# A running sum whose flag is replaced by a second address read from a table

## The reference

```python
q, k, v = x @ Wq + bq, x @ Wk + bk, x @ Wv + bv      # 6250 nodes, 8 heads of 32
e = edge_attr @ We                                    # 106250 edges, sorted by dst
alpha = sum_c(q[dst] * (k[src] + e)) / sqrt(32)
ea = exp(alpha - segment_max(alpha, dst)[dst])
denom = segment_sum(ea, dst)
out = segment_sum((v[src] + e) * ea / denom[dst], dst) + x @ Ws + bs
```

## Time and profile before

| | us |
|---|---|
| median of 3 runs | 2572.81 (2572.0 to 2574.0) |
| the profiled execution: its own time | 2570.37 |
| the profiled execution: first to last instruction | 2568.6 |
| busy: PE | 2382.9 |
| busy: DVE | 2037.0 |
| busy: POOL | 1811.8 |
| busy: ACT | 1577.5 |

### The profile page before, as it was taken

The page is one execution under the profiler, slowest core; times in us unless marked ns, Lnnn a source line. Parts: engine busy times, 40 slices in busy tenths (PEclk is TensorE's granted clock), DMA queues, the critical chain, the costliest instruction groups (busy, mean ns, idle before and its releaser), DMA issues. The chain is left out here.

```text
span 2568.6 us, 67072 instructions
## 1 busy us (share of the span) xinstructions
PE 2382.9 (93%) x13310; PEld 1992.2 (78%) x13311; DVE 2037.0 (79%) x5261; ACT 1577.5 (61%) x4373; POOL 1811.8 (71%) x2136
## 2 busy tenths in 40 slices
PE   6998999999999999999999999999995657999998
PEld 2445788888888888888888888888883646999998
DVE  6865899999999999999999999999997773222222
ACT  1222677777777677777767777767774224666665
POOL 4123788888888888888888888888886104666666
PEclk9999999999999999999999999999998557999999
DMA  7326777777777777777777777777772753433443
GB/s 229 128 107 187 231 227 221 227 228 228 223 227 227 220 230 224 221 227 226 227 221 226 227 225 229 227 218 220 228 223 78 227 162 60 71 63 64 70 66 55
DMA packets 337693, 476.68 MB, mean 186 GB/s; under 512 B 61318, under 2 KB 268492, under 8 KB 337052
## 3 DMA queue, kind: packets, MB, share of 16 engines
q0 software_dynamic: 92576, 259.72, 37.8%
q1 hardware_dynamic: 238492, 213.23, 28.0%
q10 hardware_dynamic: 6288, 0.05, 0.1%
HBM read 425.40 MB, written 50.57 MB: 185 GB/s over the span
## 5 line engine op out<-in xcount | busy, mean ns | idle before, releaser
L809 POOL DMA_INDIRECT kv_ring<-vk_table,tab_c x880 | 860.6, 978 | 284.3 <-issue 208.2
L963 PE MATMUL ps_e<-we_sb,aT 128*128 128x256 f32 x3520 | 919.5, 384 | 27.9 <-DVE ve_ke L1050 21.6
L963 PEld LDWEIGHTS ps_e<-we_sb,aT 128*128 128x128 f32 x3520 | 601.0, 191 | 102.8 <-issue 48.6
L1044 DVE TENSOR_TENSOR ve_ke<-kv_ring,ps_e 128x512 f32<-128x512 f32 x880 | 599.9, 682 | 38.1 <-PE ps_e L967 24.0
L1014 PE MATMUL ps_u<-ve_ke,sel 128*128 128x264 f32 x1760 | 547.7, 393 | 20.3 <-DVE node_slots L1114 6.8
L819 POOL TENSOR_TENSOR ve_ke<-ve_ke 128x256 f32<-128x256 f32 x880 | 553.4, 633 | 18.5 <-ACT factor L936 4.9
L967 PE MATMUL ps_e<-q_slots,selT 128*128 x1760 | 517.6, 375 | 0.0
L896 ACT COPY aT<-ps_t 128x256 f32<-128x256 f32 x880 | 325.5, 370 | 310.1 <-PE ps_t L951 189.6
L1114 DVE SCALAR_TENSOR_TENSOR node_slots<-node_slots,same_tile,ps_u 128x264 f32 x880 | 423.0, 481 | 29.5 <-DVE node_slots L1099 10.6
L967 PEld LDWEIGHTS ps_e<-q_slots,selT 128*128 128x128 f32 x1760 | 335.1, 190 | 45.9
L1032 DVE TENSOR_REDUCE alpha<-ve_ke 128x8 f32<-128x256 f32 x880 | 365.3, 415 | 5.6 <-issue 3.6
(11 more groups left out here) (249 smaller groups left out, 2642.3 us busy)
## 6 DMA issues: line engine op xcount, KB each, us to landing
a_ring<-in_edge_attr SPq DMA_DIRECT2D x880, 128.0 KB
loc_c<-loc_table SPq DMA_DIRECT2D x220, 128.0 KB
kv_ring<-vk_table,tab_c POOLq DMA_INDIRECT x880
vk_table<-kv_out SPq DMA_DIRECT2D x49, 256.0 KB
skip_table<-skip_out SPq DMA_DIRECT2D x49, 128.0 KB
skip<-skip_table SPq DMA_DIRECT2D x7, 896.0 KB, 10.8
xn_table<-node_slots SPq DMA_DIRECT2D x7, 896.0 KB, 6.5
out<-node_slots SPq DMA_DIRECT2D x1, 6144.0 KB
```

What stands on the lines that cost most here:

```text
L809: g.indirect_dma_start(out=kv_ring[:, i % N_KV, :], out_offset=None, in_=vk_table, in_offset=bass.IndirectOffsetOnAxis(ap=tab_c[:, c % N_T ...
L963: t.matmul(ps_e[i % 2][:, 0:D], aT[i % 2][:, k * P:(k + 1) * P], we_sb[:, k, :], start=(k == 0), stop=(k == KD - 1))
L1044: v.tensor_tensor(ve_ke[:, to:ke + 1:ke - to, 0:D], kv.rearrange("p (t d) -> p t d", t=2), e[:, None, :].to_broadcast([P, 2, D]), ALU.add) ...
```

## The change

The add becomes a plain addition. Its first operand gets an address of its own: the slot of the item's node tile where that tile goes on, and an area of 264 zeros behind the last slot where an item is the first of its node tile. The address comes from a second table of one number per item, `item_sums_from`, kept in another partition of the same tile as the first table. The register read between L1044 and L1032 is done twice per item, once for each table. `same_tile` is still made, later in the first stage, since the new table and the softmax need it; the new table takes two more operations there, and POOL clears the zeros once. `block_expert` moves into a free row of the same tile.

```diff
+        item_sums_from = item_rows[64:65, :]
...
-            q_slots = sb("q_slots", [P, NT + 2, SLOT], F32R, first_use)
-        node_slots = sb("node_slots", [P, NT + 2, SLOT])
+            q_words = sb("q_words", [P, (NT + 2) * SLOT + UW], F32R, first_use)
+        sums_flat = sb("node_words", [P, (NT + 2) * SLOT + UW])
+        ZEROS = NT + 2
...
+                g.memset(sums_flat[:, ZEROS * SLOT:], 0.0).then_inc(first_cleared, 1)
...
                 def masks(step):
                     if step == 0:
                         dve.wait_ge(turned_copied, IB)
+                        v.memset(same_tile[:, 0:1], 0.0)
+                        v.tensor_tensor(same_tile[:, 1:IT], node_tile_rep[:, 1:IT], node_tile_rep[:, 0:IT - 1], ALU.is_equal)
...
                     elif step == 2:
                         v.tensor_tensor(mask, m_lo, m_hi, ALU.add).then_inc(tables_ready, 1)
+                        dve.wait_ge(tables_ready, MASK)
+                        then(v.scalar_tensor_tensor(out=t_rep[:, :], in0=node_tile_rep[:, :], scalar=-float(ZEROS), in1=same_tile[:, :],
+                                                    op0=ALU.add, op1=ALU.mult))
+                        v.tensor_scalar(item_sums_from, t_rep[64:65, :], float(ZEROS), None, ALU.add)
...
-                def add(c, i, n, before):
+                def sums_from(c, i):
+                    return dve.value_load(item_sums_from[0:1, bass.ds(c * CH + i, 1)], min_val=0, max_val=ZEROS)
+
+                def add(c, i, n):
                     m = c * CH + i
-                    to, sofar = [sums_flat[:, bass.ds(k * SLOT, UW)] for k in (n, before)]
+                    to, sofar = [sums_flat[:, bass.ds(k * SLOT, UW)] for k in n]
                     dve.wait_ge(s["summed"], at("summed", m))
                     dve.wait_ge(s["acc_added"], at("acc_added", m - 1))
-                    v.scalar_tensor_tensor(out=to, in0=sofar, scalar=same_tile[:, m:m + 1], in1=ps_u[i % 2][:, 0:UW], op0=ALU.mult, op1=ALU.add
-                                           ).then_inc(s["acc_added"], 1)
+                    v.tensor_tensor(to, sofar, ps_u[i % 2][:, 0:UW], ALU.add).then_inc(s["acc_added"], 1)
...
-                            tiles.append(node_tile_of(c - b, k))
+                            tiles.append((node_tile_of(c - b, k), sums_from(c - b, k)))
```

More of the change, by code:

```diff
@@ L103, in gnn_ffn @@
         put_i = sb("put_i", [P, NB], I32)
-        block_expert_rows = sb("block_expert_rows", [1, NB], I32)
-        block_expert = block_expert_rows[0:1, :]
+        block_expert = item_rows[96:97, 0:NB]
         with ExitStack() as first_use:
-            q_slots = sb("q_slots", [P, NT + 2, SLOT], F32R, first_use)
-        node_slots = sb("node_slots", [P, NT + 2, SLOT])
+            q_words = sb("q_words", [P, (NT + 2) * SLOT + UW], F32R, first_use)
+        sums_flat = sb("node_words", [P, (NT + 2) * SLOT + UW])
+        ZEROS = NT + 2
+        q_slots, node_slots = [w[:, 0:(NT + 2) * SLOT].rearrange("p (j w) -> p j w", w=SLOT) for w in (q_words, sums_flat)]
         q_first, q_second = [q_slots[:, 1:NT + 2, k * D:(k + 1) * D] for k in range(2)]
-        q_moving = [q_slots[:, :, :].rearrange("p j w -> p (j w)")[:, SLOT + k * D:] for k in range(2)]
+        q_moving = [q_words[:, SLOT + k * D:(NT + 2) * SLOT] for k in range(2)]
         x_sb = node_slots[:, 1:NT + 1, D:2 * D]
-        sums_flat = node_slots[:, :, :].rearrange("p j w -> p (j w)")
         values, counts = node_slots[:, 0:NT, 0:D], node_slots[:, 0:NT, D:UW]
@@ L123, in gnn_ffn @@
         carried = sb("carried", [P, NCH], F32, c_soft)
-        same_tile = sb("same_tile", [P, IT], F32, c_soft)
         N_TAB = 4
@@ L174, in gnn_ffn @@
             stepped = sb1("stepped", [NT, IT])
+            same_tile = sb1("same_tile", [P, IT])
             node_tile_rep = sb1("node_tile_rep", [P, IT])
@@ L368, in _ @@
                         resets()
-                pool.wait_ge(first_cleared, 1)
+                pool.wait_ge(first_cleared, 2)
             @block.scalar
@@ L505, in _ @@
                 then(v.memset(q_slots[:, NT + 1, 0:2 * D].bitcast(F32), 0.0))
-                v.memset(same_tile[:, 0:1], 0.0)
-                then(v.tensor_tensor(same_tile[:, 1:IT], node_tile_rep[:, 1:IT], node_tile_rep[:, 0:IT - 1], ALU.is_equal))
                 def floats(step):
@@ L1136, in emit @@
                             n = tiles.pop(0)
-                            before = last_tile[0] if last_tile else n
+                            before = last_tile[0] if last_tile else n[0]
                             if i == 0:
                                 rescale(c - back, before)
-                            add(c - back, i, n, before)
-                            last_tile[:] = [n]
+                            add(c - back, i, n)
+                            last_tile[:] = [n[0]]
                 over_chunks(dve, emit, what="add", parts={3: "scan", 4: "scan_back", 6: "own", 7: "least", 8: "shift"})
```

## The result

The changed kernel takes 3137.7 us (median of 4 runs, 3135.1 to 3141.3), against 2573.4 before: ratio 1.219, 95% interval 1.217 to 1.222. The direction was as forecast; the amount was 564 us where 157 had been forecast. The profiled execution took 3141.3 us with a span of 3139.4.

A forecast was written before the change was run, and what follows sets the result against it. DVE was taken to bound the loop, with PE close behind and its sequencer's read at the edge of being paid. 2570.4 + 138 (chunks) + 18 (tail) + 1 (first stage) = 2727, median 2730 us, 6.1% slower; range 2640 to 2795.

The forecast's parts named there:

- A register read costs it 304, 190 and 23 ns: DVE's sequencer between L1044 and L1032: load, arithmetic and check, 0.517 us; with steps 0.63 us per whole read.
- the chain: DVE's sequencer in plain items: two reads 1.26 us plus 0.58 to the next read, 1.84 us between L1032 starts.
- third rival: In the loop, the sequencer's chain and PE's softmax lumps add up in full: 42 us more, 2772 us; chance 0.14.
- the nine plain items: Positions 1, 2, 5, 8 to 12 and 14 of a chunk, at 1.84 us each: 16.6 us.
- the two scan items: Chunk items where DVE's engine has 0.33 us more work: 1.93 us each, 3.9 us together.
- `own` and `least`: Chunk items where the sequencer waits for DVE's own result: 3.1 us for `own`, 2.7 for `least`.
- the rescaling: The chunk's `rescale` item: 1.86 us from L1032 to the next read, plus 0.10 and 1.26, 3.2 us.
- the turn of the chunk: Positions 15 to 1, across the chunk boundary: 2.5 us to position 0's L1050, then 1.7, together 4.2 us.
- the 36 that I took from PE's idle time: Loop gain from the shorter add, limited by PE's idle time: some 36 us over the loop's 1743 us.
- A hidden second read: Rival: DVE's second register read is covered, so the shorter add counts up to PE's limit: 2537 us; chance 0.07.
- cheap second read: Rival: DVE's second read costs 0.34 us; plain items gain, reads behind a waiting sequencer lose 42 us: 2580; chance 0.09.
- The first stage: Two more operations over 880 columns, 1.1 us each, mostly covered by PE's projections: +1 us, or +3 uncovered.

The follow-up runs named there:

- two short reads: Changed kernel with both tables in partition 0 and both register reads without bounds, so only their loads remain: 2561.7 us, ratio 0.995 to the kernel before.
- the packed version: Changed kernel with one unbounded read per item bringing node tile plus 128 times the slot, taken apart before the add: 2584.9 us, ratio 1.005 to the kernel before.

## Why the prediction was wrong

**The bound was read rightly.** The read lies between L1044 and L1032 on DVE's queue, and the engine starves when it is longer than L1044 covers. The changed kernel's 214.0 us of issue before the reduction show it, and the two short reads, which are covered, show it from the other side: 2562 us instead of 2762 with nothing changed but the length of the reads. That the one read was already paid by a hair in the loop before is not seen in the time: without its bounds the kernel gained 7 us, no more than the tail was to give.

**The failed step: "A register read costs it 304, 190 and 23 ns", taken for both reads.** The price came from a trace in which all of DVE's loads in the loop are from partition 0. In the changed kernel each load crosses partition 64 and takes 521 to 524 ns. The bounds, 0.34 to 0.70 us for the second read, left that out, and they left the first read untouched, though it became longer too. By the chain, 2 x 0.22 = 0.44 us in each of 880 items is 387 us; measured between the two placements were 375.

**The rest of the sum held.** With the price put right by placement the forecast's 2730 us stand beside 2762. Of it: the chain 1.84 us, measured 1.84; the part after the scores +18, for which the placement in partition 0 gives 644.7 - 626.9 = 17.8; the scores +138, measured there +171.2, from these rows of its operation L1051:

```profile
L1051 DVE TENSOR_TENSOR ve_ke<-kv_ring,ps_e x880: 672/680/689, 231.1 to 2114.5; 128x512 f32<-128x512 f32 x176
```

(2114.5 - 231.1 = 1883.4, against 1712.2.) That is 3.2 us per chunk instead of 2.6. The time is nearer to the third rival's 2772, in which the lumps in PE's work add up in full, but the trace doesn't show its mechanism: DVE's first operation waited for PE once in 1000 us. Two rows of DVE's groups with both tables in partition 0, 500 to 1500 us:

```profile
L1051 DVE TENSOR_TENSOR ve_ke<-kv_ring,ps_e 128x512 f32<-128x512 f32 x466 | 316.9, 680 | 1.2 <-PE ps_e L974 1.2
...
L1106 DVE TENSOR_TENSOR node_words<-node_words,factor 128x8 f32 x29 | 15.4, 531 | 0.0
```

From one reduction to the next, on the mean of chunks 3 to 51, the nine plain items take 17.0 us (16.6 in the forecast's sum), the two scan items 4.2 (3.9), `own` and `least` 5.7 (5.8), the rescaling 3.4 (3.2) and the turn of the chunk 4.1 (4.2). The rescaling grew because its second operation, L1106, takes 531 ns where it took 194 before.

**The shorter add.** 480 to 420 ns, as forecast. It was worth 23 us where it stood alone, and the 36 that I took from PE's idle time were too many. With two full reads it lies off the chain and gives nothing: the version that reads twice and keeps the long add takes 2741.8 us, the one with the short add and both tables in partition 0 takes 2762.2. Most of these 20 us stand in the item with the rescaling (3.06 us there, 3.41 here).

**The rivals.** A hidden second read (2537) is refuted for full reads: two of them in one partition cost 170 to 190 us. The Trainium skill (Advanced Engine Details and Errata, Sequencer Loop and Engine Queue Depths) has other engine instructions queued while the sequencer works and a queue of 8 on VectorE. The trace agrees in part: when the first load of an item begins, at 1205.2, L1056 is under way and L1123 and L1050 are already in stock, and DVE works through them until 1206.35. But the reduction stands behind both reads on the queue, it starts at 1206.91 when they are done, and DVE is idle for 0.56 us. The "cheap second read" is true of reads without bounds, and came out better than the 2580 given to it: 2562.

**The first stage** was forecast at +1 us and the loop began 7.2 us later. The kernel with two short reads is the same program up to the loop as the one with both tables in partition 0, and its loop began at 239.8 where that one's began at 231.1. So 7.2 us from one execution each can't be put down to the change. Part of it may be: in the five profiled executions with the old first stage the loop began at 229.5 to 232.4, in the eleven with the new one at 231.1 to 239.8. In the first 120 us TensorE's granted clock was, on the mean of that stretch, 0.97 of its full 2.4 GHz in the changed kernel and in the one with two short reads, and 1.00 in the kernel before and in the one that began at 231.1. The clock alone doesn't settle it, as it was 0.99 in the packed version, whose loop began at 239.1.

**The rescaling.** Its two operations on DVE took 565 and 194 ns on the mean before and 714 and 556 after, without any change in them. The second one, before and after, and one case of it beside POOL's multiplication L825:

```profile
L1099 DVE TENSOR_TENSOR node_slots<-node_slots,factor x32: 151/154/573, 502.7 to 1470.0; 128x8 f32 x32
```

```profile
L1105 DVE TENSOR_TENSOR node_words<-node_words,factor x25: 160/573/579, 500.8 to 1489.6; 128x8 f32 x25
```

```profile
1201.36 0.71 POOL L825 TENSOR_TENSOR ve_ke<-ve_ke 128x256 f32<-128x256 f32 x1
1201.53 0.57 DVE L1105 TENSOR_TENSOR node_words<-node_words,factor 128x8 f32 x1
```

In the whole changed kernel 52 of its 55 executions began while L825 was under way; each of them took 571 to 579 ns and ended 26 to 30 ns after it. The other three took 153 to 160. Before, 6 of 55 met POOL's multiplication, and those took 572 to 579. With both tables in partition 0 it mostly met POOL's gather L816 instead: 39 of 55 began 0.38 us into one, took 606 to 618 ns and ended 0 to 16 ns after it; six that began within its first 0.13 us took 155 to 163. The ends agree with an operation that is held until POOL's is over, and the new pace of the items moved it there. No run moved it by itself.

## What to carry to other kernels

An operation that costs its engine nothing can still cost its sequencer more than a vector instruction: ask what lies between two instructions on the queue, how much of it the one in flight covers, and at which waiting instruction the sequencer stands still. A second register read cost seven times what the shorter add saved by itself (170 us against 23). Keep all tables that one engine reads into registers in one half of the partitions, and leave out the check of a number that cannot be out of bounds; and take a price from a row only together with the circumstances of the row.

## What was not expected of the hardware

In the loop a load of one number from SBUF into a register of DVE takes 296 to 344 ns behind a load from the same side of partition 64 (pairs 0 and 0, 1, 8, 32, 63; 64 and 96) and 512 to 553 ns behind one from the other side (pairs 0 and 64, 32 and 64). It does not matter whether the two follow at once or an item later. The Trainium skill (SBUF — State Buffer, Specifications (TRN2)) puts partition 64 at the address 0x0100_0000, where the address bits above the lowest 24 change. That these bits decide agrees with all nine placements; the runs do not show what in the sequencer has to be set anew. Each engine's first load in the program is slow too: 553 ns on DVE, 490 on PE and 484 on ACT in the kernel before. PE, whose loads in the loop are all from partition 0, stood at 302 ns there in the changed kernel and at 301 before; its one crossing, from 0 to 96, cost 490.
